# Moving three pieces of an mLSTM stage: gate products, a mask comparison and GpSimd's query staging

## The reference, cut to what matters

```python
log_fg = log_sigmoid(fg)
cs = cumsum(log_fg, axis=2)
log_D = where(ltr, cs - swapaxes(cs_shift, -2, -1), -inf) + swapaxes(ig, -2, -1)
max_log_D = max(log_D, axis=-1)
D = exp(log_D - max_log_D)                       # 64 x 64 for each head and sequence
qk = einsum('bhsd,bhtd->bhst', qh, kh / sqrt(DH))
C = qk * D
normaliser = maximum(abs(sum(C, axis=-1)), exp(-max_log_D))
h = einsum('bhst,bhtd->bhsd', C / (normaliser + EPS), vh)
h_norm = (h - mean(h)) / sqrt(var(h) + LN_EPS) * (1.0 + out_w)
x = x + h_norm                                   # first layer
...
mask = arange(s)[None, :] < x_seqlens[:, None]   # third layer, keys beyond a length are shut out
```

## Time and profile before

| | |
|---|---|
| median of 3 runs | 1232.23 us |
| the profiled execution's own time | 1232.76 us |
| its span in the trace | 1231.0 us |
| PE busy | 1027.4 us (83%) |
| DVE busy | 855.5 us (69%) |
| ACT busy | 576.6 us (47%) |
| POOL busy | 222.0 us (18%) |
| mLSTM loop, `exponents(0)` to `heads(7)` | 39.54 to 99.96 us |

### The profile page before, as it was taken

One profiled execution on the slowest core, in us unless ns is written; L12 is line 12 of the kernel. 1 busy time (PEld: TensorE's weight loads), 2 busy tenths in 40 slices (PEclk: granted clock), 3 DMA queues, 4 the chain that ended last, 5 costly groups with the idle time before them and its releaser, 6 DMA issues.

```text
span 1231.0 us, 32393 instructions
## 1 busy us (share of the span) xinstructions
PE 1027.4 (83%) x11974; PEld 816.6 (66%) x11974; DVE 855.5 (69%) x1903; ACT 576.6 (47%) x1119; POOL 222.0 (18%) x243
## 2 busy tenths in 40 slices
PE   5678999969888886899899999899998673798756
PEld 5357888746556566778678877678776562467546
DVE  5565677788999996555677676687675577667455
ACT  1223344556666663343555665465655220344343
POOL 3554122100111101331100000000000122343100
PEclk9877999989999998899999999999999885699778
DMA  9200000000000000000000000000000000000001
GB/s 369 95 2 1 0 0 0 0 2 2 0 0 0 0 0 2 2 1 1 2 2 0 0 0 2 2 1 0 0 0 2 1 0 0 1 1 0 1 0 34
DMA packets 5919, 16.13 MB, mean 13 GB/s; under 512 B 729, under 2 KB 4962, under 8 KB 5218
## 3 DMA queue, kind: packets, MB, share of 16 engines
q1 hardware_dynamic: 5858, 15.29, 3.2%
HBM read 14.24 MB, written 1.05 MB: 12 GB/s over the span
## 4 chain that ended last, share of the span: by engine, by line
PE 40%; issue 23%; DVE 18%; DVEq 11%; POOL 3%; ACT 2%; POOLq 2%; PEldq 1%; PEld 1%; ACTq 0%
PE banks L1674 7%; PE banks L1747 4%; PE banks L1719 3%; PE banks L1136 3%; PE banks L900 3%; PE banks L1707 3%; DVEq L1346 2%; PE banks L1358 2%; PE banks L1117 1%; PE banks L1735 1%; DVE small L1591 1%; DVE xn L333 1%; POOL small L832 1%; DVEq L1012 1%; DVE xr L1011 1%
## 5 line engine op out<-in xcount | busy, mean ns | idle before, releaser
L352 POOL TENSOR_TENSOR rstd<-var,nhalf 128x2 f32<-128x2 f32 x72 | 57.3, 796 | 483.0 <-DVE var L326 483.0
L1682 ACT ACTIVATE work<-banks 128x512 f32<-128x512 f32 x128 | 74.9, 600 | 70.2 <-PE banks L1674 70.2
L1339 ACT ACTIVATE work<-work 128x1024 f32<-128x1024 f32 x64 | 67.7, 1058 | 55.6 <-DVEq L1335 32.0
L374 ACT ACTIVATE xT_all<-banks 128x256 f32 (+1 forms) x72 | 28.3, 393 | 133.5 <-PE banks L363 133.0
L1674 PE MATMUL banks<-xT_all,weights 128*128 (+1 forms) x384 | 86.2, 380 | 2.3 <-ACT work L1792 1.8
L1358 PE MATMUL banks<-ident,work 128*128 128x128 f32 x512 | 71.0, 290 | 16.2 <-DVE work L1349 11.2
L1674 PEld LDWEIGHTS banks<-xT_all,weights 128*128 128x128 f32 x384 | 71.5, 190 | 13.7 <-ACT work L1792 2.6
L929 ACT ACTIVATE work<-banks,weights 128x256 f32<-128x256 f32 x128 | 53.6, 470 | 57.5 <-PE banks L890 56.5
L1358 PEld LDWEIGHTS banks<-ident,work 128*128 128x128 f32 x512 | 62.9, 150 | 23.3 <-DVE work L1349 13.3
L1826 DVE TENSOR_TENSOR work<-banks,neg_mask 128x512 f32<-128x512 f32 x64 | 40.7, 685 | 52.2 <-PE banks L1707 50.6
L363 PE MATMUL banks<-ident,xn 128*128 128x128 f32 x144 | 33.6, 320 | 43.7 <-DVE xn L333 38.4
(11 more groups left out here) (311 smaller groups left out, 2413.3 us busy)
## 6 DMA issues: line engine op xcount, KB each, us to landing
weights<-wpack SPq DMA_DIRECT2D x1, 5381.5 KB, 32.1
weights<-wpack SPq DMA_DIRECT2D x1, 2060.0 KB, 13.2
weights<-wpack SPq DMA_DIRECT2D x1, 2049.0 KB, 17.5
weights<-wpack SPq DMA_DIRECT2D x1, 1160.5 KB, 19.8
x_all<-x_in SPq DMA_DIRECT2D x2, 512.0 KB, 4.8
ctxT_all<-ctxT_in SPq DMA_DIRECT2D x1, 1024.0 KB, 7.0
out<-x_all SPq DMA_DIRECT2D x8, 128.0 KB, 1.8
rows<-rows_in SPq DMA_DIRECT2D x1, 832.0 KB
```

What stands on the lines that cost most here:

```text
L352: g.tensor_tensor(rstd, var, nhalf[:, 0:2], ALU.pow).then_inc(rstd_ready, 1)
L1339: act.activation(sm[:, u, :], sm[:, u, :], ACT.Exp, scale=scale).then_inc(h["exp"].sem, 1)
L1682: act.activation(dst.rearrange("p c t -> p (c t)"), bank(ring.bank(f"qk{c}")), ACT.Copy) \
```

## The change

Four edits in the mLSTM stage and the opening:

- On PE, `products(p)` now stands ahead of `exponents(p)`, both before the loop and in it. The table `scans` gives the PSUM banks in that order too.
- On DVE, the comparison that makes `neg_len` moves from the end of the opening to behind the gate scans, right ahead of `decayed(0)`.
- On POOL, `queries(p+2)` and `spread(p+2)` move from the head of iteration p to its end, behind the product with the weights.

```diff
-        scans = [[(f"arg{p}", "a"), (f"qa{p}", "v"), (f"qb{p}", "v")] for p in range(PAIRS)]
+        scans = [[(f"qa{p}", "v"), (f"qb{p}", "v"), (f"arg{p}", "a")] for p in range(PAIRS)]
...
             v.tensor_scalar(neg_mask[:], mask_u8, -NEG, None, ALU.mult)
-            v.tensor_tensor(neg_len[:].rearrange("p (b k) -> p b k", k=S),
-                            iseq[:, None, :].to_broadcast([P, B, S]),
-                            lensf[:, :, None].to_broadcast([P, B, S]), ALU.is_ge)
...
             pe.wait_ge(rows_taken, 1)
+            products(0)
             exponents(0)
-            products(0)
...
                     if p == 0:
                         pe.wait_ge(em_made, 1)
+                    products(p + 1)
                     exponents(p + 1)
-                    products(p + 1)
...
+            masks(0)
             decayed(0)
...
             for p in range(PAIRS):
-                if p + 2 < PAIRS:
-                    queries(p + 2)
-                    spread(p + 2)
                 g.wait_ge(*hvar_made.at(p, 1))
...
                                 lstm_ow.rearrange("p (u d) -> p u d", u=2), ALU.mult).then_inc(weighted.sem, 1)
-                if p + 2 == PAIRS:
+                if p + 2 < PAIRS:
+                    queries(p + 2)
+                    spread(p + 2)
+                elif p + 2 == PAIRS:
                     stage_inputs(g, moe0, 0)
```

More of the change, by code:

```diff
@@ L689, in lstm_vector, with masks @@
             s = lstm
-            def masks():
-                v.tensor_scalar(neg_len[:], neg_len[:], -NEG, None, ALU.mult)
-                v.drain().then_inc(converted, 1)
+            def masks(part):
+                if part == 0:
+                    v.tensor_tensor(neg_len[:].rearrange("p (b k) -> p b k", k=S),
+                                    iseq[:, None, :].to_broadcast([P, B, S]),
+                                    lensf[:, :, None].to_broadcast([P, B, S]), ALU.is_ge)
+                else:
+                    v.tensor_scalar(neg_len[:], neg_len[:], -NEG, None, ALU.mult)
+                    v.drain().then_inc(converted, 1)
             def decayed(p):
@@ L772, in lstm_vector @@
                 elif p == 0:
-                    masks()
+                    masks(1)
                 scale(p)
```

## The result

The changed kernel took 1251.48 us (median of 4 runs, 1248.86 to 1252.98), the kernel before 1232.1 us (median of 4). The ratio is 1.0163 with a 95% interval from 1.0134 to 1.0193, that is 20 us slower, 16.5 to 23.8. The forecast was 1253.5 us.

The account below looks back on a forecast made before the run. Bound by a chain of waits, 7.29 us a pair, no engine full; after the change a staging loop. `heads(1)` 6.0 us late, five periods of 11.0 us make 21.3 us: 1232.2 + 21.3 = 1253.5 us, range 1243.5 to 1259.

Parts of the forecast that it names:

- the rival with all matmuls slow: mLSTM loop: the loop over the staging binds with every matmul slow, 11.68 us a period; 1257.6 us, chance 18%.
- the one with all fast: mLSTM loop: the loop over the staging binds with every matmul fast, 9.37 us a period; 1244.1 us, chance 8%.
- The step that the index behind POOL's rows is one lower: POOL, mLSTM loop: behind pair p's weights now comes staging for p+2, not p+3, so `heads(p+1)` waits; 9.37 to 11.68 us.
- The terms of the loop: Start-to-start times from `heads(p)` over POOL's staging to `heads(p+1)`: eight terms, summing to 9.37 us fast, 11.68 us slow.
- The mix of the matmuls' two speeds: mLSTM loop: slow `products` and `exponents`, `heads` fast in two of three periods, slow in one; 11.0 us a period.
- The opening: Before the loop: `products(0)` runs in PE's wait ahead of `exponents(0)`, so `heads(0)` comes 1.29 us earlier, at 46.4.
- The cover of `decayed`: mLSTM loop: `decayed` ends 1.66 us behind `exponents`, the sums come 1.75 us behind, so it is hidden by 0.1 us.
- The mask: DVE's comparison of 2.29 us, moved ahead of `decayed(0)`: 2.3 to 3.5 us there, no cost up to `heads(0)`.
- paid once: mLSTM loop: staging for pair 2 comes 6 us late, then POOL with its idle 2.41 us catches up; 1238 us, 6%.
- the two that saw no loss: mLSTM loop: staging leaves DVE's way, 0.74 us a period, 1227.2 us, 3%; or staging hidden in other waits, 1230.9 us, 3%.

## Why the prediction was right

The time came out 2.0 us below the forecast; the rival with all matmuls slow was 6.1 us above it, the one with all fast 7.4 us below.

- The step that the index behind POOL's rows is one lower, and so a loop over the staging arises: shown, by the move alone and by undoing it alone.
- The terms of the loop: 1.17 from `heads` to ACT (67.03 to 68.20), 0.21, 1.30, 3.07 from `pow` to `queries` (69.71 to 72.78), 1.14 on to `products` (I took 1.25), 1.44 for `products` with its drain (I took 1.36), 1.91, and 0.37 for the turn. That is 10.61 us, and the period that began and ended so was 10.60 us. With slow heads and turn it was 11.66 us (forecast 11.68).
- The mix of the matmuls' two speeds: the five periods from `heads(1)` to `heads(6)` came to 55.8 us, 11.16 each, against 11.0. Slow heads stood at the start of three of the five (once they took 1.54 us, between the two speeds), not of one in three. No row gave that share; I took it from the look of a few periods, and that the mean came within 0.16 us is in part luck. The page "TensorE: Matmul & The Clock Gate" of the Trainium skill (Part 1, the HAM clock gate), by whose rule the prediction had all slow, was right for `products` and `exponents`, slow in each of the six periods with a wait (1.13 and 1.98 us), but not for the heads, fast in two of the five.
- One reading behind that mix doesn't hold up. I took the two speeds for the two levels of the granted clock, but the profile gives 1.00 for every microsecond from 39 to 46 us before the change, and there `exponents` took 1.97 and 1.98 us. The sum is not hurt, since its terms are durations.
- The opening was mis-sized: `heads(0)` came 2.57 us earlier instead of 1.29. `products` and `exponents` of pair 1 took 0.82 and 1.08 us where before had 1.13 and 1.98, which is 1.2 us of the rest. This and the longer periods cancelled in part: at `heads(6)` the delay is 72.47 - 51.51 = 21.0 us against 21.3.
- The cover of `decayed`: in the trace it held from `heads(1)` on, at `heads(2)` by 0.16 us (0.1 was forecast); at `heads(0)`, which has no turn and came fast, the chain ran over `decay` and `decayed` instead, and the sums started 0.28 us behind ACT's absolute value instead of 0.21.
- The mask: no cost that can be told, 3.02 us long in the range of 2.3 to 3.5.
- The rival "paid once" and the two that saw no loss fell with the period of 11 us.

## What to carry to other kernels

A move in a loop's code may keep the row order of an engine and yet lower the index behind it by one: count for each hand-off how many iterations the maker leads the taker, and treat a lead that falls to zero as a new loop whose whole length must be summed. An engine that idles ahead of a step gains nothing when work is taken away from in front of it. Once such a loop binds, each instruction in it is worth its time once per iteration, and work beside it, such as `products` beside `spread`, begins to matter, though it was worth nothing measurable before.

## What the runs showed of the hardware

- The mask comparison took 2.29 us alone and 3.02 us beside POOL's copies, and the copy of 1024 elements that ran into it (L811) 2.91 us instead of 1.03. The copy started at 41.65 us, DVE ended at 43.66, and the copy 0.90 us later: it seems to have stood still until DVE was done. The Trainium skill's page "SBUF — State Buffer" (SBUF: two separate sides) calls the shared pair of ports an exclusive lock: the engine that starts first has it for its whole instruction, and the other waits. The trace agrees with that.
- Behind the drain that ends `products`, PE stood still for 0.31 to 0.36 us ahead of the next matmuls in the changed kernel, and for 0.16 to 0.42 us in the kernel before.
- The granted clock could be high through a pause and fall at its end, as the single microseconds above show (1.00 at 72 us with PE idle, 0.50 at 73 us). More PE work in the pause made `products` fast in three periods of six, but not the `heads` behind them.
- Granted clock and duration need not agree: the same `exponents` took 1.97 us at 38.95 and 1.08 us at 43.52 in the changed kernel, both at a granted clock of 1.00. The durations are the safer guide to the speed.
